# Half of a short convolution on TensorE, and three smaller pieces moved, in a fused attention and feed-forward kernel

## The chip, the cores and the metric

One core of one Trainium2 chip. The metric is the device time of one execution in microseconds, the median of the runs.

## The reference

Input x is 4 batches of 256 tokens by 256 channels. Each layer half starts with a bidirectional weighted scan over time (its keys and values are a second input, `fside`), and the two halves are a state-space block and a quantised feed-forward block:

```python
# scan, for two sets of weights: forward and reverse recurrences a = a*decay + ek*v, b = b*decay + ek
out = sigmoid(r) * (nf + nb - ekv + euk * vf) / max(df + db - ek + euk, 1e-8) * (0.8 + 0.2 * tf)
# state-space block
z, x, B_proj, C_proj, dt_logits = split(u @ in_proj_w)
x = silu(causal_conv1d(x, conv_weight, conv_bias))        # 4 taps, 512 channels
y = ssd(q=elu(C)+1, k=elu(B)+1, v=x, a=exp(-dt*exp(A_log))) + D_param * v      # 8 heads of 64
y = rms_norm(y) * norm_scale * silu(z);  x = x + y @ out_proj_w
# feed-forward, both matmuls with 8-bit activations and ternary weights
h = layer_norm(gelu(silu(bitlinear158(scan2, w1, b1)))) * g + b
x = x + bitlinear158(h, w2, b2)
```

## The kernel before

Every engine has a program of its own, a hand-written list of calls of small functions at the end of its block; semaphores (`wait_ge`, `then_inc`) join them. All order is in these lists and in `HOME`, which says in which of the 8 PSUM banks each piece lies. A batch b is 256 tokens, two tiles c of 128; the feed-forward works on 8 tiles i.

- SP issues the loads, then per batch `spread_sums(b)` (6 small transfers of the running sums), the transposing transfers `turn_q2(i)` and the stores.
- DVE does the scans: `forward(b, w, k)` and `backward(b, w, k)`, w for the two weight sets, k for denominator and numerator; `add_own`, `recip`, `ratio`, and `gated(b)`, which makes uT, the input of the batch's projections. ACT makes the exponentials (`wkv_exp`, `wkv_own`), the decays D and the seed of the reciprocal; POOL multiplies by the values (`times_v`, `own_times_v`).
- PE projects uT: `features(b)` (B, C and dt), `conv_in(b, i)` (x, two channel blocks of 128 each), `gate_in(b, c)` (z). The convolution runs with channels on the partitions: `conv_last_tap` (ACT) writes cv = x times the last tap plus bias, `conv_taps(b, i)` (DVE) adds the three earlier taps in 6 operations for each i, and `conv_turns(b, c)` (PE) turns the 4 blocks of a tile to tokens on the partitions. ACT's `silu_conv` makes vv.
- `softplus_out(b)` (DVE) gives la, the log decays; `running_sums(b)` (PE, ACT, DVE) and `spread_sums(b)` make the operands of `log_decays(b, c, g)` (PE); ACT's `decays` takes the exponential, DVE's `attend` multiplies by the scores.
- `within(b, c)` (PE) first adds the skip (8 matmuls against `skips`, identities scaled by D_param, made once by ACT), then 8 matmuls with dec. `y_turns`, `project(p)` and `residual(p)` end the block. p counts parts: batches 0 to 2, then the last batch's two tiles as parts 3 and 4.
- `norm_h`, `ffn_in_scale`, `quantise_h`, `q1_turns` quantise. `ffn_up(i)` multiplies by w1T and adds the bias through `diag` (POOL, 1/al1 on the diagonal; 1/al1 from DVE's `ffn_in_back`) times b1b, b1 broadcast to 128 partitions. `ffn_silu`, `ffn_gelu`, `ffn_var`, `ffn_center`, `ffn_shift`, `ffn_max`, `ffn_round` follow, then `turn_q2(i)` and `ffn_down(i)`; DVE's `ffn_back(i)` makes the output scale al2.

## Time and profile before

| | |
|---|---|
| median of 3 runs | 205.26 us (204.13 to 205.44) |
| profiled execution, first to last instruction | 201.1 us |
| instructions | 3190 |
| mean granted clock of TensorE | 0.924 |

The time of a run is taken from outside the program, the span inside it; of the profiled execution the span is all that is known. "Busy" is time in which an engine has an instruction under way; for PE the ends of matmuls are modelled, so the distance between starts tells more than the printed duration. A 32-bit matmul shows as two records. The timelines print start, duration, engine, line, operation, output and input tiles, and the idle time before with what ended it.

### The profile page before, as it was taken

Reading aid. Unit: us, or ns where it says so; the run is one execution under the profiler, and the core shown is the slowest. Engines: PE = TensorE matmul, PEld = TensorE weight load, DVE = VectorE, ACT = ScalarE, POOL = GpSimd, SP = SyncE. Lnnn points to the kernel's source line nnn. Section 1 sums busy time; section 2 is a strip of 40 time slices with the busy share of each in tenths; the row PEclk is TensorE's granted clock in tenths of the full one; section 3 lists DMA queues with packets and bytes.
Section 4 is the critical chain, followed back from the end, with each engine's and each line's share of the span. In section 5 each row is a group of like instructions: output and inputs, shape, how many; then the busy total and the mean of one; then the engine's idle time right before and its main releaser. Section 6 shows DMA issues by size and latency. Waiting matters only on the chain.

```text
span 201.1 us, 3190 instructions
## 1 busy us (share of the span) xinstructions
PE 159.6 (79%) x903; PEld 117.4 (58%) x908; DVE 178.6 (89%) x320; ACT 159.8 (79%) x293; POOL 100.3 (50%) x172
## 2 busy tenths in 40 slices
PE   7800039459799999999999999999999999672844
PEld 5600038334589867698757488957668766350633
DVE  2899999999999999899999899979866769998991
ACT  5860599969699279998789999899999886877632
POOL 3609759000426523758700086467455287858570
...
GB/s 133 320 385 382 248 2 104 106 3 2 1 0 3 0 0 2 4 3 0 2 2 3 0 0 3 0 2 0 54 96 14 0 0 0 130 7 49 81 60 96
DMA packets 12304, 11.55 MB, mean 57 GB/s; under 512 B 7680, under 2 KB 10368, under 8 KB 12032
## 3 DMA queue, kind: packets, MB, share of 16 engines
...
q8 instruction: 7, 0.11, 0.2%
...
## 4 chain that ended last, share of the span: by engine, by line
PE 45%; DVE 14%; ACT 12%; issue 12%; POOL 8%; DMA 5%; SPq 3%; POOLq 1%; DVEq 0%; ACTq 0%
PE banks L1688 41%; DVE Ys L1239 5%; DMA wn<-wn 4%; PE banks L1685 3%; DVE Fs L1230 3%; DVE nd L1250 3%; SPq L355 2%; ACT Ys L744 1%; POOL qr L514 1%; ACT Ys L742 1%; POOL wn L576 1%; ACT dec L691 1%; ACT dec L844 1%; ACT D L724 1%; DMA cum_t<-cum_s 1%
## 5 line engine op out<-in xcount | busy, mean ns | idle before, releaser
L1688 PE MATMUL banks<-inw,uT 128*128 128x8 f32 (+1 forms) x64 | 21.7, 465 | 19.4 <-DVE uT L1277 19.4
L1688 PEld LDWEIGHTS banks<-inw,uT 128*128 128x128 f32 x64 | 10.9, 217 | 24.7 <-issue 24.5
L1230 DVE TENSOR_TENSOR_SCAN Fs<-D,E 128x514 f32<-128x514 f32 x16 | 23.0, 1460 | 0.5 <-POOL D L449 0.5
L1688 PE MATMUL banks<-uT,inw 128*128 128x256 f32 x80 | 20.3, 398 | 0.0
L1239 DVE TENSOR_TENSOR_SCAN Ys<-D,Fs 128x514 f32<-128x514 f32 x16 | 19.7, 1250 | 0.0
L1323 DVE SCALAR_TENSOR_TENSOR cv<-banks,cols,cv 128x255 f32<-128x255 f32 (+2 forms) x48 | 19.4, 472 | 0.1
L1688 PEld LDWEIGHTS banks<-uT,inw 128*128 128x128 f32 x80 | 15.2, 197 | 4.2 <-issue 2.1
L508 POOL TENSOR_TENSOR vs<-vv,grow 128x512 f32<-128x512 f32 x4 | 4.5, 1121 | 25.8 <-issue 20.3
L1688 PEld LDWEIGHTS banks<-vv,skips 128*128 128x128 f32 x128 | 15.2, 192 | 1.9 <-issue 1.8
L495 POOL TENSOR_TENSOR own<-own,vT 128x1024 f32<-128x1024 f32 x4 | 12.1, 3025 | 8.4 <-DVE own L1220 8.4
L1688 PE MATMUL banks<-vv,dec 128*128 128x64 f32 x128 | 15.6, 275 | 0.0
L1688 PE MATMUL banks<-vv,skips 128*128 128x64 f32 x128 | 15.3, 273 | 0.0
L1688 PE MATMUL banks<-b1b,diag 128*128 128x512 f32 x32 | 15.0, 592 | 0.0
L1688 PE MATMUL banks<-outw,yzT 128*128 128x256 f32 x64 | 15.0, 382 | 0.1
L1688 PEld LDWEIGHTS banks<-vv,dec 128*128 128x128 f32 x128 | 14.9, 192 | 0.0
L501 POOL TENSOR_TENSOR nd<-nd,Ys 128x512 f32<-128x512 f32 x4 | 5.2, 1301 | 17.5 <-DVE Ys L1261 17.5
L1688 PE MATMUL banks<-w2T,wn 128*128 128x256 f16 x64 | 9.0, 290 | 6.0 <-DMA wn<-wn 6.0
L1688 PE MATMUL banks<-starts 128*128 128x256 bf16 x80 | 12.1, 317 | 1.3 <-POOL starts L429 1.3
L1688 PEld LDWEIGHTS banks<-outw,yzT 128*128 128x128 f32 x64 | 11.8, 190 | 2.3 <-issue 0.5
L742 ACT ACTIVATE Ys<-nd 128x1024 f32<-128x1024 f32 (+1 forms) x5 | 4.4, 885 | 9.9 <-DVE nd L1250 9.9
L930 ACT ACTIVATE wn<-wn,grs 128x1024 f16<-128x1024 f32 x8 | 9.2, 1146 | 2.6 <-DVE wn L1443 1.5
L1347 DVE TENSOR_TENSOR dec<-dec,banks 128x1024 f32<-128x1024 f32 x8 | 9.7, 1210 | 1.7 <-ACT dec L844 1.7
...
## 6 DMA issues: line engine op xcount, KB each, us to landing
...
```

The source lines that it names most:

```text
L495: pool.tensor_tensor(own[:, b % 2, :, 1, :], own_e(b), vT[:, b].unsqueeze(1).broadcast_to([P, 2, CT * T]), ALU.mult)\
L501: pool.tensor_tensor(nd[:, 1, 1], nd[:, 1, 1], rn[:, 1], ALU.mult).then_inc(rat2_ok, 1)
L508: pool.tensor_tensor(by_head(vs[:]), by_head(vv[:, b % 2, 0]), grow[:, 0, :].unsqueeze(2).broadcast_to([P, NH, HD]), ALU.mult).then_inc(vs ...
L742: act.activation(seed, den, ACT.Relu, bias=-DEN_FLOOR).then_inc(rl_ok, 1)
L930: act.activation(Q2[:, i % 2], Y[:, i % 2], ACT.Square, scale=grs[:, i:i + 1], accum_out=qss[:, i:i + 1])\
L1230: dve.tensor_tensor_scan(Fs[:, w, k], D[:, w, 0:CT * TS], E[:, b % 2, k].rearrange("p c t -> p (c t)"), 0.0, ALU.mult, ALU.add).then_inc(f ...
L1239: dve.tensor_tensor_scan(Ys[:, w, k][:, ::-1], D[:, w, 1:CT * TS + 1][:, ::-1], Fs[:, w, k][:, ::-1], 0.0, ALU.mult, ALU.add).then_inc(ys_ ...
L1250: last = dve.scalar_tensor_tensor(nd[:, :, w, s], y, gap[:, w, ct, b:b + 1], own[:, b % 2, w, :, s], ALU.mult, ALU.add)
L1323: dve.scalar_tensor_tensor(cv[:, ft, back:], at("conv_in", b, i)[:, j * T:(j + 1) * T - back], cols[:, w:w + 1], cv[:, ft, back:], ALU.mul ...
L1347: dve.tensor_tensor(dec[:, c], dec[:, c], at("scores", b)[:, c * P:(c + 1) * P].unsqueeze(1).broadcast_to([P, NH, P]), ALU.mult).then_inc( ...
L1685: return pe.transpose(dst, src, ident[0:n, 0:n])
L1688: return pe.matmul(dst, lhsT, rhs, start=start, stop=stop)
```

## The change

- **Convolution.** Channel blocks 2 and 3 (`conv_in(b, 1)`) go another way: ACT copies them raw into `xps`, which has 3 zero columns ahead, and `conv_turns` multiplies shifted slices of xps with `taps`, 8 diagonal matrices made once by POOL, so that the sum over taps and the turn are one accumulation in PSUM; the bias comes in by a matmul of one row of ones with one row `convb`. Blocks 0 and 1 stay as they were.
- **Skip.** POOL multiplies vv by D_param (`skip_values`), and `within` adds it with one matmul of 512 columns against the identity. ACT's `make_skips` goes.
- **Bias of ffn_up.** b1 and the factor 1/al1 are each split in three 16-bit pieces (`bias_piece` on ACT and `bias_rest` on POOL for b1; `bias_factors` on POOL, `factor_turns` on PE, `factor_rows` on ACT for the factor); the product is one 16-bit matmul over 67 rows.
- **Tile scales.** al1 and al2 are made by POOL (in `bias_factors`, `ffn_round`). DVE's `ffn_in_back` and `ffn_back` go. Statistics have a column per tile, so that some waits go.
- **Lists and banks.** All lists and `HOME` are new, the loads' order too. `gate_x` writes over xcT, `crest` shares bcr.

```diff
 HOME = {
-    "conv_turns": ((2, 3), (7, 2), (1, 0), (7, 6)),
+    "conv_turns": ((2, 4), (7, 1), (4, 4), (5, 6)),
...
+            def make_taps():
+                pool.wait_ge(ident_ok, 2)
+                pool.wait_ge(cols_in, 16)
+                for j in range(2):
+                    for k in range(TAPS):
+                        w = R_CV + k * FT + 2 + j
+                        last = pool.tensor_scalar(taps[:, j, k], ident[:], cols[:, w:w + 1], 1.0, ALU.mult, ALU.mult)
+                last.then_inc(taps_ok, 1)
...
+            def bias_factors(p):
+
+                s = tiles_of(p)
+                pool.wait_ge(hr_ok, 2 * p + 2)
+                pool.wait_ge(hq_ok, p + 1)
+                pool.wait_ge(wmean_ok, 3)
+                for i in range(s.start, s.stop):
+                    pool.tensor_scalar(fac[:, i:i + 1], hmv[:, i:i + 1], hr[:, i:i + 1], wrec[:, 0:1], ALU.mult, ALU.mult)
+                    last = pool.tensor_scalar(al1[:, i:i + 1], hm[:, i:i + 1], hr[:, i:i + 1],
+                                              (wmean if i < FIRST_TANH else whalf)[:, 0:1], ALU.mult, ALU.mult)
+                last.then_inc(al1_ok, 1)
+                pool.wait_ge(al1_ok, p + 1)
+                for k in range(3):
+                    n = 6 * p + 2 * k + 2
+                    if k == 0:
+                        pool.tensor_tensor(fact[:, s], fac[:, s], hq[:, s], ALU.mult).then_inc(fac_ok, 1)
+                    else:
+                        pool.tensor_tensor(fact[:, s], fact[:, s], fpc[:, s, 0, k - 1], ALU.subtract).then_inc(fac_ok, 1)
+                    pool.wait_ge(fac_ok, n)
+                    pool.tensor_scalar(fpc[:, s, :, k], fact[:, s].unsqueeze(2).broadcast_to([P, s.stop - s.start, 3]),
+                                       1.0, 0.0, ALU.mult, ALU.add).then_inc(fac_ok, 1)
+                    if k < 2:
+                        pool.wait_ge(fac_ok, n + 1)
...
+            def skip_values(b, c):
+                pool.wait_ge(heads_in, 16)
+                pool.wait_ge(vv_ok, TT * b + c + 1)
+                if b >= 1:
+                    pool.wait_ge(y_ps, TT * (b - 1) + c + 1)
+                pool.tensor_tensor(by_head(skv[:, c]), by_head(vv[:, b % 2, c]),
+                                   heads[:, 2, :].unsqueeze(2).broadcast_to([P, NH, HD]), ALU.mult).then_inc(sk_ok, 1)
...
+            def conv_raw(b):
+                act.wait_ge(xp_ps, 2 * b + 1)
+                act.wait_ge(pads_ok, 1)
+                if b >= 1:
+                    act.wait_ge(cvT_ps, TT * b)
+                act.activation(xps[:, :, PAD:], halves(at("conv_in", b, 1)), ACT.Copy).then_inc(raw_ok, 1)
...
+            def factor_rows(p):
+                s = tiles_of(p)
+                act.wait_ge(fT_ps, p + 1)
+                act.activation(fT[:, s.start * P:s.stop * P], at("factor_turns", p)[0:KB, 0:(s.stop - s.start) * P],
+                               ACT.Copy).then_inc(fT_ok, 1)
...
             def conv_turns(b, c):
+                bank = at("conv_turns", b, c)
+                pe.wait_ge(ones_ok, 1)
+                pe.wait_ge(b_in, 48)
+                pe.wait_ge(taps_ok, 1)
+                pe.wait_ge(raw_ok, b + 1)
+                mm(bank[:, 2 * P:], ones[NS:NS + 1, :], convb, True, False)
+                for j in range(2):
+                    for k in range(TAPS):
+                        mm(bank[:, (2 + j) * P:(3 + j) * P], xps[:, j, c * P + k:(c + 1) * P + k], taps[:, j, k], False,
+                           j == 1 and k == TAPS - 1)
                 pe.wait_ge(ident_ok, 2)
-                pe.wait_ge(tap_ok, 4 * PAD * (b + 1))
-                turn_4(at("conv_turns", b, c), [cv[:, ft, c * P:(c + 1) * P] for ft in range(FT)]).then_inc(cvT_ps, 1)
+                pe.wait_ge(tap_ok, 2 * PAD * (b + 1))
+                for ft in range(2):
+                    last = turn(bank[:, ft * P:(ft + 1) * P], cv[:, ft, c * P:(c + 1) * P])
+                last.then_inc(cvT_ps, 1)
...
             def within(b, c):
                 bank = at("within", b, c)
-                pe.wait_ge(cumi_ok, 2)
+                pe.wait_ge(ident_ok, 2)
+                pe.wait_ge(sk_ok, TT * b + c + 1)
+                mm(bank, ident[:], skv[:, c], True, False)
                 pe.wait_ge(vv_ok, TT * b + c + 1)
-                for h in range(NH):
-                    part = slice(h * HD, (h + 1) * HD)
-                    mm(bank[:, part], skips[:, h], vv[:, b % 2, c, part], h == 0, False)
...
             def ffn_up(i):
...
-                pe.wait_ge(dg_ok, i + 1)
+                pe.wait_ge(fT_ok, part_of(i) + 1)
+                pe.wait_ge(b1_ok, 5)
                 for g in range(2):
                     half = slice(g * 512, (g + 1) * 512)
-                    last = mm(ffn_mid(i)[:, half], diag[:, i % 2], b1b[:, half], False, True)
+                    last = mm(ffn_mid(i)[:, half], fT[:, i * P:(i + 1) * P], b1r[:, half], False, True)
```

PE where batch 0's turns end and batch 1 begins (`taps,xps` are the tap diagonals, `uT,inw` conv_in and the B and C features, `vs,sc` is between). Before:

```order
L1688 MATMUL banks<-never,identb 128x512
L1688 MATMUL banks<-cum_t,cum_s 128x512
L1685 MATMUL banks<-ident,cv 128x128 x4
L1688 MATMUL banks<-never,identb 128x512
L1688 MATMUL banks<-cum_t,cum_s 128x512
L1688 MATMUL banks<-never,identb 128x512
L1688 MATMUL banks<-cum_t,cum_s 128x512
L1688 MATMUL banks<-uT,inw 128x256 x4
L1688 MATMUL banks<-inw,uT 128x8 x4
L1688 MATMUL banks<-uT,inw 128x256 x2
L1688 MATMUL banks<-vv,skips 128x64 x8
L1688 MATMUL banks<-vv,dec 128x64 x8
```

Now:

```order
L1735 MATMUL banks<-bcf,ones 128x256
L1735 MATMUL banks<-taps,xps 128x128 x8
L1732 MATMUL banks<-ident,cv 128x128 x2
L1735 MATMUL banks<-never,identb 128x512
L1735 MATMUL banks<-cum_t,cum_s 128x512
L1735 MATMUL banks<-inw,uT 128x8 x4
L1735 MATMUL banks<-uT,inw 128x256 x10
L1735 MATMUL banks<-vs,sc 128x512
L1735 MATMUL banks<-tri,la 72x128 x2
L1735 MATMUL banks<-bcf,ones 128x256
L1735 MATMUL banks<-taps,xps 128x128 x8
L1732 MATMUL banks<-ident,cv 128x128 x2
```

Each tile's turns now carry the ones row and 8 diagonals; features(1) stands ahead of both conv_in(1, .), and the running sums and first turns of batch 1 come before within(0, 0), not after it.

DVE from the first scan to the first log decays la (`Fs` forward, `Ys` backward scan, `nd` add_own, `tn` and the Ys after it recip, `uT` gated). The first rows before:

```order
L1230 SCALAR_TENSOR_TENSOR Fs<-D,E 128x514
L1173 TENSOR_SCALAR decay<-fdec,eew 128x3 x4
L1180 TENSOR_SCALAR gap<-decay 128x4x3
L1182 SCALAR_TENSOR_TENSOR gap<-decay,gap 128x4x3
L1184 TENSOR_SCALAR gap<-gap 128x4x3
L1230 SCALAR_TENSOR_TENSOR Fs<-D,E 128x514 x2
L1239 SCALAR_TENSOR_TENSOR Ys<-D,Fs 128x514
L1220 TENSOR_SCALAR own<-own 128x2x512
L1239 SCALAR_TENSOR_TENSOR Ys<-D,Fs 128x514
L1230 SCALAR_TENSOR_TENSOR Fs<-D,E 128x514
```

Now:

```order
L1285 TENSOR_SCALAR D<-starts,decay 128x256 x4
L1304 TENSOR_SCALAR E<-E 128x2x256
L1318 SCALAR_TENSOR_TENSOR Fs<-D,E 128x514
L1308 TENSOR_SCALAR own<-own 128x2x512
L1318 SCALAR_TENSOR_TENSOR Fs<-D,E 128x514 x2
L1261 TENSOR_SCALAR decay<-fdec,eew 128x3 x4
L1268 TENSOR_SCALAR gap<-decay 128x4x3
L1270 SCALAR_TENSOR_TENSOR gap<-decay,gap 128x4x3
L1272 TENSOR_SCALAR gap<-gap 128x4x3
L1327 SCALAR_TENSOR_TENSOR Ys<-D,Fs 128x514 x2
```

The minimum of E of batch 1 now stands ahead of the first scan, the own minimum right behind it, and the decays of the other batches behind three scans instead of one.

PE in the tail (`outw,yzT` is project(4), `b1b,diag` and `b1r,fT` the bias of ffn_up, `w2T,wn` ffn_down, `identb,fpc` factor_turns). Before:

```order
L1688 MATMUL banks<-outw,yzT 128x256 x4
L1685 MATMUL banks<-ident,h 128x128 x2
L1688 MATMUL banks<-wcol,less 128x256
L1688 MATMUL banks<-w2T,wn 128x256 x8
L1688 MATMUL banks<-wcol,less 128x256
L1688 MATMUL banks<-w2T,wn 128x256 x8
L1688 MATMUL banks<-w1T,q1T 128x512 x4
L1688 MATMUL banks<-b1b,diag 128x512 x2
L1685 MATMUL banks<-ident,h 128x128 x2
L1688 MATMUL banks<-wcol,less 128x256
L1688 MATMUL banks<-w2T,wn 128x256 x8
```

Now:

```order
L1735 MATMUL banks<-outw,yzT 128x256 x4
L1735 MATMUL banks<-identb,fpc 67x128
L1735 MATMUL banks<-wcol,less 128x256
L1735 MATMUL banks<-w2T,wn 128x256 x8
L1735 MATMUL banks<-w1T,q1T 128x512 x4
L1735 MATMUL banks<-b1r,fT 128x512 x2
L1732 MATMUL banks<-ident,h 128x128 x2
L1735 MATMUL banks<-identb,fpc 67x128
L1735 MATMUL banks<-wcol,less 128x256
L1735 MATMUL banks<-w2T,wn 128x256 x8
L1735 MATMUL banks<-w1T,q1T 128x512 x4
L1735 MATMUL banks<-b1r,fT 128x512 x2
```

Only ffn_down(1) stands between project(4) and ffn_up(6), and ffn_up(7) comes ahead of ffn_down(3).

## Rows read from the trace of the kernel before

**Rows 1.** The page, part 1: busy us of each engine.

```profile
PE 159.6 (79%) x903; PEld 117.4 (58%) x908; DVE 178.6 (89%) x320; ACT 159.8 (79%) x293; POOL 100.3 (50%) x172
```

**Rows 2.** Busy us of PE, PEld, DVE, ACT, POOL by stage; PE clock; DMA.

```profile
56.00:168.70 112.70, 112.08 (x638) 84.54 (x642) 101.24 (x187) 101.13 (x185) 55.81 (x96) 1.00 0.04 8
168.70:201.10 32.40, 18.70 (x124) 12.60 (x124) 26.39 (x49) 18.83 (x33) 20.65 (x47) 0.95 0.27 66
```

**Rows 3.** The chain that ended last: start us, us, what.

```profile
46.42 0.80 SPq L355
...
50.01 1.69 DMA cum_t<-cum_s
...
55.98 14.31 PE banks L1688 x96
```

**Rows 4.** Timeline of PE, 72 to 102 us: start us, us, operation.

```profile
72.82 0.93 PE L1688 MATMUL banks<-bcf 64*128 64x128 f32 x6
73.68 0.39 PE L1688 MATMUL banks<-la,late 128*128 128x8 f32 x2
...
81.05 0.38 PE L1688 MATMUL banks<-never,identb 128*128 128x512 bf16 x1
81.30 0.38 PE L1688 MATMUL banks<-cum_t,cum_s 99*128 99x512 bf16 x1
...
83.82 1.96 PE L1688 MATMUL banks<-uT,inw 128*128 128x256 f32 x8
...
87.37 1.89 PE L1688 MATMUL banks<-vv,skips 128*128 128x64 f32 x16
89.10 1.95 PE L1688 MATMUL banks<-vv,dec 128*128 128x64 f32 x16
...
94.46 1.08 PE L1688 MATMUL banks<-yy,ident 128*128 128x512 f32 x2
95.38 0.60 PE L1685 MATMUL banks<-ident,nd 128*128 128x128 f32 x4
95.81 0.60 PE L1688 MATMUL banks<-tri,la 128*72 128x128 f32 x4
96.25 0.60 PE L1685 MATMUL banks<-ident,h 128*128 128x128 f32 x4
...
101.87 1.88 PE L1688 MATMUL banks<-b1b,diag 128*128 128x512 f32 x4
```

**Rows 5.** Timeline of DVE (and one of ACT), 7 to 88 us.

```profile
7.06 2.34 DVE L1230 TENSOR_TENSOR_SCAN Fs<-D,E 128x514 f32<-128x514 f32 x1 [0.53 <-POOL D L449]
...
7.07 0.63 ACT L703 ACTIVATE E<-vT 128x512 f32<-128x512 f32 x1 [0.28 <-DMA vT<-in_kT_dram]
...
26.84 1.56 DVE L1277 SCALAR_TENSOR_TENSOR uT<-th,nd 128x512 f32<-128x512 f32 x1
...
41.94 0.38 DVE L1311 SCALAR_TENSOR_TENSOR la<-dtp,expa 128x72 f32<-128x72 f32 x2
...
55.17 0.66 DVE L1277 SCALAR_TENSOR_TENSOR uT<-th,nd 128x512 f32<-128x512 f32 x1
...
86.99 2.33 DVE L1230 TENSOR_TENSOR_SCAN Fs<-D,E 128x514 f32<-128x514 f32 x2
```

**Rows 6.** Groups of DVE: busy us, mean ns, idle before.

```profile
L1323 DVE SCALAR_TENSOR_TENSOR cv<-banks,cols,cv 128x255 f32<-128x255 f32 (+2 forms) x48 | 19.4, 472 | 0.1
...
L1464 DVE TENSOR_SCALAR al<-qm,gq,wmean 128x1 f32<-128x1 f32 x8 | 2.0, 266 | 0.0
```

**Rows 7.** POOL: two groups, and one operation of its timeline.

```profile
L508 POOL TENSOR_TENSOR vs<-vv,grow 128x512 f32<-128x512 f32 x4 | 4.5, 1121 | 25.8 <-issue 20.3 <-ACT grow L809 5.5
...
L566 POOL TENSOR_SCALAR gq<-qr,grs 128x1 f32<-128x1 f32 x8 | 2.1, 264 | 0.8
...
26.16 1.70 POOL L488 TENSOR_TENSOR E<-E,vT 128x512 f32<-128x512 f32 x1 [2.35 <-DVE E L1216]
```

**Rows 8.** Timeline of ACT in the tail: tile 7's tanh.

```profile
182.27 1.12 ACT L899 ACTIVATE own<-banks,al 128x1024 f32<-128x1024 f32 x1 [0.84 <-PE banks L1688]
```

More of the change, by code:

```diff
@@ L76, in build @@
     NR = R_CV + TAPS * FT
+    KB = 64 + 3
     with ExitStack() as ctx:
@@ L985, in _ @@
+            features(1)
+            decays(0, 1, 1)
+            softplus_log(1)
+            conv_last_tap(1)
+            conv_raw(1)
+            act.preload_act_table_set("silu_and_others")
             silu_conv(0, 1)
             silu_z(0, 1)
-            cross_scores(0)
+            silu_conv(1, 0)
             act.preload_act_table_set("exp_and_others")
-            decays(0, 0, 1)
-            decays(0, 1, 0)
-            growths(0)
-            wkv_exp(3)
-            features(1)
-            decays(0, 1, 1)
@@ L995, in _ @@
-            conv_last_tap(1, 1)
-            gate_x(2)
-            wkv_own(3)
+            growths(1)
+            cross_scores(1)
+            bias_piece(1)
+            gate_x(2)
+            running_sums(1)
+            gate_x(3)
+            act.preload_act_table_set("natural_log_exp_and_others")
+            recip_seed(2, 0, 2)
+            bias_piece(2)
+            make_turn(3)
+            act.preload_act_table_set("silu_and_others")
+            silu_z(1, 0)
+            silu_conv(1, 1)
@@ L1814, in project, with factor_turns @@
                 last.then_inc(o_ps, 1)
+            def factor_turns(p):
+                s = tiles_of(p)
+                pe.wait_ge(masks_ok, 4)
+                pe.wait_ge(fac_ok, 6 * p + 7)
+                for k, i in enumerate(range(s.start, s.stop)):
+                    last = mm(at("factor_turns", p)[0:KB, k * P:(k + 1) * P],
+                              fpc[:, i].rearrange("p j k -> p (j k)")[:, 0:KB], identb[:], True, True)
+                last.then_inc(fT_ps, 1)
             def q1_turns(p):
@@ new lines, in _ @@
+            log_decays(0, 1, 1)
+            pe.wait_ge(vv_ok, 1)
+            features(1)
+            pe.wait_ge(dex_ok, 3)
+            conv_in(1, 1)
+            pe.wait_ge(zs_ok, 1)
+            conv_in(1, 0)
+            pe.wait_ge(bcr_ok, 2)
+            pe.wait_ge(dtx_ok, 2)
+            between(0)
+            running_sums(1)
+            conv_turns(1, 0)
+            pe.wait_ge(vv_ok, 2)
+            scores(1)
+            pe.wait_ge(vv_ok, 3)
+            r2_turns(1)
+            gate_in(1, 0)
@@ L1896, in _ @@
+            pe.wait_ge(ty_ok, 1)
+            gate_in(1, 1)
             within(0, 0)
-            between(0)
-            pe.wait_ge(dex_ok, 4)
+            conv_turns(1, 1)
+            pe.wait_ge(att_ok, 2)
             within(0, 1)
-            conv_in(1, 0)
+            features(2)
             y_turns(0, 0)
-            gate_in(1, 0)
-            running_sums(1)
-            scores(1)
+            log_decays(1, 0, 0)
+            conv_in(2, 1)
+            pe.wait_ge(yss_ok, 2)
+            pe.wait_ge(yz_ok, 2)
@@ L1951, in _ @@
-            conv_turns(2, 0)
-            pe.wait_ge(dex_ok, 11)
-            conv_turns(2, 1)
-            pe.wait_ge(dex_ok, 12)
-            gate_in(2, 1)
-            within(2, 0)
+            log_decays(2, 1, 1)
+            pe.wait_ge(wcol_ok, 1)
+            gate_in(2, 1)
+            pe.wait_ge(dex_ok, 10)
+            conv_turns(2, 1)
+            pe.wait_ge(dex_ok, 11)
+            within(2, 0)
+            pe.wait_ge(zs_ok, 6)
+            ffn_up(1)
+            between(2)
             pe.wait_ge(vv_ok, 6)
-            between(2)
```

959 lines of the change are left out of this document (464 added, 495 removed).

## The prediction

> **What bounds the kernel now.** I read the page's first part, then the busy time by stage, the chain that ended last, and the timelines of PE and DVE. The page gives DVE 89% of the span, PE and ACT 79% each [rows 1]; by that alone VectorE is the limit, and a change that takes work from it should pay. The stages say otherwise. From 56 to 168.7 us PE is busy 112.08 of 112.70 us at the full clock of 2.4 GHz, while DVE has 101.24 and ACT 101.13 [rows 2]. The chain agrees: from 55.98 us it runs over pieces such as 96 matmuls in a row [rows 3]. So there are three stages. Up to 56 us the DVE's scans decide when PE may start (its last step is uT of batch 1, at 55.17 [rows 5]); then 112.7 us belong to PE; then 32.4 us of tail, in which DVE, POOL, ACT and transfers hand single tiles to each other (DVE 26.39, PE 18.70 busy [rows 2]). The profiled span is 201.1 us; the median of the runs is 205.26, so some 4.2 us lie around it. I sum against the span and add the 4.2 back.
>
> **PE, part by part.** Prices are from start to start in the timeline [rows 4], a "record" being one of the two into which a 32-bit matmul falls.
> - Skip product: 8 matmuls of 64 columns per tile cost 89.10-87.37 = 1.73 us. One of 512 columns against the identity costs what yy,ident costs, 95.38-94.46 = 0.92. That is -0.81, for 8 tiles -6.5.
> - Bias: b1b,diag is printed 1.88 for 4 records, with an overlapped end of 0.16 as in yy,ident (printed 1.08, 0.92 by starts), so 1.72. Two 16-bit matmuls of 512 columns cost about 0.44 to 0.5 (one is 81.30-81.05 = 0.25), and the factor turns 0.11 a tile. That is -1.2, for 8 tiles -9.3.
> - Convolution: per tile two of four turns go (4 records of 128 columns are 95.81-95.38 = 0.43, so -0.22). In come one matmul of 256 columns (2 records at 1.96/8 = 0.245, 0.49) and 8 of 128 columns, 16 records. This is the price that decides. The trace has no such matmul over 128 rows. Below it lie the turns and tri,la (0.43 and 0.44 for 4 records, 0.11 each) [rows 4]; above it lie bcf with 6 records in 73.68-72.82 = 0.86, 0.143 each, and the 256-column record at 0.245. I take 0.115, near the rows with full width; it makes 1.84 a tile and +2.1 net, for 8 tiles +17. With 0.143 it is +20, with 0.245 +33.
> The sum on PE is +17-6.5-9.3 = about +1. The page TensorE: Matmul & The Clock Gate of the Trainium skill (Back-to-back issue gap) gives about 81 ns per matmul of N=128 in a sustained stream; the trace's full-width 32-bit records are slower, 0.11; by the page's figure the 128 added records would be 4 us cheaper in all.
>
> What of this lies in the PE stage? Conv turns of batches 1 to 3 (six tiles, +12.6 to +15), all eight skips (-6.5), biases of tiles 0 to 5 (-7), one warm-up block of 8 matmuls (it lies ahead of the stage), and the turn of ratio 1, now in the stage (+0.4): -0.5 at 0.115, +2 at 0.143. The stage had next to no idle time, so DVE's relief can't shorten it: DVE loses 24 of 48 tap operations (19.4/48 = 0.40 each, -9.7 us) and its small scale operations (8 al2 at 0.25, -2, and 13 for al1 and ral that I price alike, -3) [rows 6], 14 to 15 us in all, hidden behind PE, and ACT's gain (8 last-tap pieces less, 8 skip diagonals less) is taken back by the raw copies, bias pieces and factor rows.
>
> **The front.** Here the new lists matter. Before, the first scan is at 7.06 and la of batch 0 at 41.94 [rows 5], 34.9 us. Laid end to end in the new order: 16 scans at 2.33/2 = 1.17 [rows 5] (18.7), eight pieces around them (own minimum twice 1.2, decays and gaps 1.2, nd 2.6, two reciprocals 2.7, ratio, uT, features 2.1), and 0.3 of waits: 29 us. The difference is stalls that the old order had around the own product on POOL. But the first scan now waits for the minimum of E of batch 1, whose exponential was at 7.07, straight off the transfer [rows 5], and that transfer now has another 256 KB ahead: scan at about 8.7, +1.7. la(0) then comes at about 38, -4. The running sums follow at once (+2.2 of wait for PE and ACT) and the six spreading transfers start near 41.5 instead of 46.42 [rows 3]; they took 5.3 us to 51.7. Gated(1) has one tap group less ahead but two more pieces and a wait for the reciprocal seed; I get 54.1 for 55.8. ACT now makes its table changes one after the other here (silu_conv, growths, silu_z, features, four table loads), so la(1) is at about 61.7 and PE waits some 2 us at the running sums of batch 1. Walking on to where gate_in(1, 1) and conv_turns(1, 1) are done I arrive at 75.2 to 75.7 with 19.4 us of PE work behind, where before it was 19.7 at 75.95. So the front is worth half a microsecond at this point, since PE waits again.
>
> From there PE has 90.2 us to project(4) at 0.115 less what is taken ahead of it (ffn_down(0), q1_turns(3)), before 90.8: the stage ends 0.6 us earlier at the low price, 1.3 later at the high one. I take -0.6.
>
> **The tail.** Tile 6's project(3) stands 10.3 us of PE work ahead of project(4), before 4.3, so ffn_up(6) follows it at once. Tile 7 was the last; its tanh began at 182.27, released by PE [rows 8]. Now its bias factors go through POOL (eight small operations at 0.2 to 0.35 each, as gq's 0.264 [rows 7], about 2.5 us with their waits), one PE turn and an ACT copy that stands behind gelu(6), so ffn_up(7) is done about 1.8 us sooner than those 182.27-168.7 = 13.6 us after project(4); before its tanh ACT now does square(5), so 1.3 of it reaches the end. DVE has 2 us less in this stage, which gives 0.6 more; the al2 product on POOL between the last two roundings takes 0.3 back. Tail: -1.6. The sum is 201.1-0.6-1.6 = 198.9, with the 4.2 about 203.0.
>
> **Rivals.**
> - *DVE was the pace after all* (chance 0.24). PE's fullness would be an effect of matmuls that stretch while they wait. For it: DVE too is 90% busy in that stage, 101.24 of 112.70 us. Against: the same function costs the same on PE wherever its rows stand in the timeline. Half of the 14 us comes through: 201.1-6.5+4.2, about 198.
> - *The 32-bit weight load shows* (0.14, slower). Each added record of 128 columns carries a load of a full 128x128 block, and 0.19 us is what one takes; if it isn't hidden behind so short a matmul, a record costs 0.19: 96 records in the PE stage by 0.075 more is +7.2, some 208.5. For it: bcf at 0.143 is above the turns. Against: skips with 64 columns ran at 0.108 with the same load. It decides from 0.14 on, where the 2.2 us of gain are gone.
> - *POOL becomes a link* (0.14, slower). It gets 8 skip products at 1.12 us [rows 7], which stand between silu and within(b, c), two bias rests of 1024 columns, and five factor chains of 2 to 3.5 us, some 30 us more in a queue in order; clip_weights(1) on DVE sits behind scale_outw and weight_round(1). If each batch loses 1 to 1.5 us of PE to it, 207. While both read two operands, each slows the other: uT took 1.56 us beside POOL's 1.70 us product, 0.66 alone [rows 5, 7]. The Trainium skill's GPSIMD Engine Reference (Engine selection; Key points) warns of this: two-input elementwise work is about half as fast there and contends with VectorE instructions that have two SBUF inputs. The trace agrees.
> - *The front isn't won* (0.08): the first loads or the table changes come later than I put them, and the gain of the tail is all: 205.3 less or more 1.
>
> **How the numbers follow.** My case has 0.40 and its own range of 200.5 to 205.5. A measurement of this kernel tells about 1% from no change, 2 us, so faster is below 203.2: 0.24 of my case, 0.23 of the first rival, 0.01 of the last, 0.48. Slower is above 207.3: 0.02, 0.12 and 0.10, with 0.02 of the last, 0.26. The rest, 0.26, is no change. The range 198.0 to 208.5 leaves out the full gain of DVE's 14 us and a record price above 0.19.
>
> **What would show it.** Right: PE again full from some 54 to 168 us; starts of taps,xps 0.11 to 0.12 apart; la(0) near 38; DVE's busy time in the PE stage down by 10 us or more with the stage's length the same; the last tanh near 181. Wrong: gaps on PE released by POOL skv or by ACT vv; tap records at 0.14 or more; PE with idle time while the span falls by 5 us (then DVE was the pace); a wait of DVE for wn from POOL that PE then feels at project(0) or within(1, 0).

## The result, and the profile after

The changed kernel takes 244.68 us (median of 4 runs, 243.37 to 247.19), before in the same session 204.69 (203.39 to 205.44): the ratio is 1.1945, 95% interval [1.1866, 1.2023]. It is 40 us slower where I had forecast 203.0. The profiled execution has a span of 245.1 us and belongs to the longest of the four runs; the spans of the others are 241.6 to 243.2, so the stages below hold 2 to 3.5 us more than the others', and the gains counted from 244.68 are good to about 1 us.

The page's first part, to be held against [rows 1]:

```profile
PE 173.6 (71%) x879; PEld 125.8 (51%) x884; DVE 168.0 (69%) x276; ACT 160.1 (65%) x289; POOL 142.7 (58%) x237
```

DVE did lose its 10 us (178.6 to 168.0). PE gained 14 us, and POOL 42, part of which, as will be seen, is waiting inside its instructions. The page's time slices show where the time went (busy tenths in 40 slices of 6.1 us; the clock row is the granted one):

```profile
PE   1900009942499999599996089999999998556545
...
POOL 5469004509519043298499961077685888877780
PEclk9985555895558999859999659999999999958777
DMA  6969410000100000200000000000004000130411
```

PE is empty in the third to sixth slice (12 to 37 us; in before from 10 to 25), low from the ninth to the eleventh, and empty once more in the 23rd, in which POOL is full. The transfers at the start go on in a ragged row of 6, 9, 6, 9, 4, 1. The chain that ended last (start, us, what) names the same places:

```profile
5.77 19.91 DMA xcT<-in_xT_dram
...
57.33 7.23 POOL taps L487 x8
...
132.10 8.65 POOL fpc L531
```

In the chain of before no transfer and no group of POOL was longer than 4.2 us. To place the loss I cut each span at two PE instructions, the first of features(1) (inw,uT, 8 records) and the first of project(4) (outw,yzT, 8 records): front, PE stage, tail.

| kernel | front | stage | tail | span |
|---|---|---|---|---|
| before | 57.8 | 109.1 | 34.2 | 201.1 |
| after | 76.1 | 131.0 | 38.0 | 245.1 |

So 18.3 us are lost in the front, 22.0 in the stage (the cut differs from [rows 2] by a few us), 3.8 in the tail. The rows of each place:

The front, ACT and DVE of after:

```profile
25.71 0.63 ACT L819 ACTIVATE xcT<-xcT 128x512 f32<-128x512 f32 x1 [15.83 <-DMA xcT<-in_xT_dram]
...
31.43 0.69 DVE L1346 SCALAR_TENSOR_TENSOR tn<-nd,Ys 128x512 f32<-128x512 f32 x1 [8.05 <-ACT Ys L815]
...
49.83 0.38 DVE L1399 SCALAR_TENSOR_TENSOR la<-dtp,expa 128x72 f32<-128x72 f32 x2
```

gate_x(1) waits until 25.71 for its transfer; behind it in ACT's list stands the seed of the first reciprocal, for which DVE idles 8.05 us. la(0) comes at 49.83 for 41.94 before [rows 5] and 38 in the forecast. The wait is not all of it. Two groups of scans are longer than the 1.17 us apiece of the forecast, and each lies beside POOL's own product:

```profile
10.87 4.44 DVE L1318 TENSOR_TENSOR_SCAN Fs<-D,E 128x514 f32<-128x514 f32 x2
...
42.86 6.79 DVE L1327 TENSOR_TENSOR_SCAN Ys<-D,Fs 128x514 f32<-128x514 f32 x4
...
11.04 3.19 POOL L547 TENSOR_TENSOR own<-own,vT 128x1024 f32<-128x1024 f32 x1 [2.09 <-DVE own L1308]
...
43.07 3.26 POOL L547 TENSOR_TENSOR own<-own,vT 128x1024 f32<-128x1024 f32 x1
```

That is 2.1 us too much in each group. Then POOL and PE:

```profile
57.32 7.23 POOL L487 TENSOR_SCALAR taps<-ident,cols 128x128 f32<-128x128 f32 x8
...
64.80 1.19 PE L1735 MATMUL banks<-bcf,ones 1*128 1x256 f32 x2 [5.13 <-POOL taps L487]
65.92 3.78 PE L1735 MATMUL banks<-taps,xps 128*128 128x128 f32 x16
```

The diagonals stand behind times_v(2), which had waited 9.35 us. The group's line for L487 gives 366 ns for the shortest, 368 median and 2322 for the longest of the eight. After the gap PE runs at the granted clock of 0.5, 1.2 GHz (page slices 9 5 5 5 8): 3.78 us for 16 tap records that take 1.89 at full clock. In the stage:

```profile
126.06 2.41 DVE L1410 SCALAR_TENSOR_TENSOR cv<-banks,cols,cv 128x255 f32<-128x255 f32 x6
128.38 1.22 DVE L1327 TENSOR_TENSOR_SCAN Ys<-D,Fs 128x514 f32<-128x514 f32 x1
129.52 1.20 DVE L1318 TENSOR_TENSOR_SCAN Fs<-D,E 128x514 f32<-128x514 f32 x1
130.64 0.67 DVE L1454 TENSOR_TENSOR yy<-banks,zs 128x512 f32<-128x512 f32 x1
...
132.33 1.21 DVE L1327 TENSOR_TENSOR_SCAN Ys<-D,Fs 128x514 f32<-128x514 f32 x1
...
137.94 2.70 DVE L1338 SCALAR_TENSOR_TENSOR nd<-Ys,gap,own 128x512 f32<-128x512 f32 x4
...
128.38 2.41 POOL L519 TENSOR_SCALAR fac<-hmv,hr,wrec 128x1 f32<-128x1 f32 x1
...
131.48 0.23 POOL L531 TENSOR_SCALAR fpc<-fact 128x6 bf16<-128x6 f32 x1
...
132.10 8.64 POOL L531 TENSOR_SCALAR fpc<-fact 128x6 bf16<-128x6 f32 x1
```

Two instructions of the same form, six elements a partition: 0.23 us at 131.48, 8.64 at 132.10. The long one begins as DVE enters an unbroken row of scans and sums and ends at 140.74, when that row ends (137.94+2.70 = 140.64). The 2.41 us of fac at 128.38 cover two scans and end as DVE turns to an instruction that reads PSUM. PE waits 8.77 us for it.

### The profile page after: what moved, and what is told of

It reads as the page before. It is cut to its first block, busy times and chain, and to the rows that moved or that the text cites. A ratio compares the mean times of both kernels' runs of the same rounds, so it can differ in the third digit from the quotient of the medians.

```text
span 245.1 us, 3178 instructions
## 1 busy us (share of the span) xinstructions
PE 173.6 (71%) x879; PEld 125.8 (51%) x884; DVE 168.0 (69%) x276; ACT 160.1 (65%) x289; POOL 142.7 (58%) x237
## 3 DMA queue, kind: packets, MB, share of 16 engines
q1 hardware_dynamic: 11782, 11.09, 15.3%
HBM read 8.44 MB, written 1.05 MB: 39 GB/s over the span
## 4 chain that ended last, share of the span: by engine, by line
PE 30%; POOL 24%; issue 13%; DVE 11%; ACT 10%; DMA 9%; SPq 2%; POOLq 1%; DVEq 0%; ACTq 0%
PE banks L1735 28%; DMA xcT<-in_xT_dram 8%; POOL fpc L531 5%; POOL taps L487 3%; POOL own L547 3%; PE banks L1732 2%; POOL fac L519 2%; DVE Ys L1327 1%; DVE nd L1338 1%; DMA wn<-wn 1%; POOL h L598 1%; POOL wn L633 1%; DVE banks L1507 1%; POOL E L540 1%; SPq L320 1%
## 5 line engine op out<-in xcount | busy, mean ns | idle before, releaser
L1735 PE MATMUL banks<-uT,inw 128*128 128x256 f32 x80 | 23.4, 446 | 0.0
L1735 PEld LDWEIGHTS banks<-uT,inw 128*128 128x128 f32 x80 | 17.6, 226 | 4.7 <-issue 1.2
L1735 PEld LDWEIGHTS banks<-taps,xps 128*128 128x128 f32 x128 | 18.0, 224 | 3.3 <-issue 3.3
L1735 PE MATMUL banks<-taps,xps 128*128 128x128 f32 x128 | 19.6, 316 | 0.0
L1735 PE MATMUL banks<-w2T,wn 128*128 128x256 f16 x64 | 12.2, 355 | 4.5 <-DMA wn<-wn 4.5
L1374 DVE SCALAR_TENSOR_TENSOR bcf<-banks,bcr 64x256 f32<-64x256 f32 x8 | 3.4, 421 | 15.8 <-ACT bcr L835 15.6
L1465 DVE SCALAR_TENSOR_TENSOR x<-banks,yr,xn 128x256 f32<-128x256 f32 x8 | 3.6, 480 | 15.3 <-PE banks L1735 15.3
L1338 DVE SCALAR_TENSOR_TENSOR nd<-Ys,gap,own 128x512 f32<-128x512 f32 x16 | 13.5, 897 | 0.0
L1346 DVE SCALAR_TENSOR_TENSOR tn<-nd,Ys 128x1024 f32<-128x1024 f32 (+1 forms) x5 | 5.0, 1007 | 11.9 <-ACT Ys L815 11.9
L819 ACT ACTIVATE xcT<-xcT 128x512 f32<-128x512 f32 x4 | 2.5, 622 | 15.8 <-DMA xcT<-in_xT_dram 15.8
L531 POOL TENSOR_SCALAR fpc<-fact 128x6 bf16<-128x6 f32 (+1 forms) x15 | 11.9, 797 | 1.4
## 6 DMA issues: line engine op xcount, KB each, us to landing
inw<-in_in_w_dram SPq DMA_DIRECT2D x1, 1160.0 KB, 20.5
```

Source lines behind the costliest of these rows:

```text
L531: pool.tensor_scalar(fpc[:, s, :, k], fact[:, s].unsqueeze(2).broadcast_to([P, s.stop - s.start, 3]), 1.0, 0.0, ALU.mult, ALU.add).then_in ...
L1338: last = dve.scalar_tensor_tensor(nd[:, :, w, s], y, gap[:, w, ct, b:b + 1], own[:, b % 2, w, :, s], ALU.mult, ALU.add)
L1346: dve.scalar_tensor_tensor(tn[:, w0:w1], nd[:, 0, w0:w1], DEN_FLOOR, rd[:, w0:w1], ALU.max, ALU.mult)\
L1735: return pe.matmul(dst, lhsT, rhs, start=start, stop=stop)
```

## The experiments

Labels e and h change the kernel after, f the kernel before, g goes from e8 back. The medians of before that were measured beside them are 203.8 to 204.9 us. "Front, stage, tail" are cut as above. Each quoted block is what I expected before the run.

**Three waits mended one by one.** e1 moves one ACT call (which costs two more table loads), e2 one POOL call, e3 adds memsets on DVE, e4 is all three.

```diff
 e1, ACT:   gate_x(0)
-           gate_x(1)
            ...
            recip_seed(0, 1, 2)
            ...
+           gate_x(1)
 e2, POOL:
+           make_taps()
            times_v(2)
-           make_taps()
 e3, DVE:   backward(3, 0, 1)
+           rest(0)      # dve.memset(pause[:, 0:1], 0.0)
            forward(3, 1, 0)
+           rest(1)
            ...
```

> One part of the new ACT list undone: gate_x(1), which waited for the DMA of xcT until 25.71 us and held the seed of the first reciprocal behind it, stands behind recip_seed(0,1,2) again, with the table loads it needs there (two more, 1.28 us each, on ACT). Theory (the front is lost to one queued wait): DVE's idle 8.05 us before tn at 31.43 shrinks to under 2.5 us, uT(0) comes near 29.5 to 31 instead of 35.89, la(0) near 44 instead of 49.83, and the total falls by 3 to 6 us from 244.7. Rival (the front is lost to the loads themselves, or what is won there is taken back by the taps' wait at 57 to 65): uT(0) moves by less than 2 us, or it moves and the total falls by less than 1.5 us.

> Only POOL's list changes: make_taps stands ahead of times_v(2) instead of behind it, where POOL was idle 9.35 us. Theory A (POOL is starved of a port that it shares with DVE, and the eight products took 7.23 us because of that): beside the scan block 43 to 49.5 they take 4 us or more as well, but end before 56; the wait of PE on taps (5.13 us) goes, features(1) starts 4 to 6 us sooner than 76.06, and the total falls by 4 to 7 us. Theory B (each such product simply takes 0.9 us on POOL): the same 7.2 us for eight, ended by 54, the same gain. What tells A from B is the spread of the eight durations: A has 0.3 to 0.4 us for those beside an idle DVE or one that reads PSUM and over 1 us beside scans, B has 0.9 for each. Theory C (the wait at 59.6 hid another, such as cv0 or tap): PE's gap stays over 3 us and the total moves by less than 1.5 us.

> After with six one-column memsets of 0.1 us put on DVE between the scans and sums of 132 to 141 us (after backward(3,0,1), forward(3,1,0), forward(3,1,1), backward(3,1,0), backward(3,1,1), add_own(3,0)). Theory A (POOL's tiny fpc instruction of 8.64 us waited for the shared port, which DVE's instructions with two SBUF inputs handed to each other without a gap; a memset, which reads nothing, lets POOL in): the 8.64 us falls below 3 us, PE's wait of 8.77 us to under 3, and the total falls by 5 to 8 us although DVE has six instructions more. Theory A2 (the port is what POOL waits for, but a memset doesn't hand it over): fpc stays near 8.6 and ends where DVE's block ends. Rival B (the 8.64 us is a hiccup of POOL itself, such as loading code, not DVE's doing): it stays as long at the same place whatever DVE runs, and its end no longer falls together with the end of DVE's block.

> The edits of e1, e2 and e3 together. Theory (the 40 us are a few queued waits, each about 5 to 9 us, and all the arithmetic of the change was priced nearly right): the three add up, 244.7 falls to 222 to 230. Rival (each gain runs into the next wait of the same chain): under 10 us in all, 235 or more.

e1: 237.12 us, -7.6, more than expected; uT(0) at 28.60, la(0) at 44.47. e2: 240.43, -4.3; the eight durations are 368 ns at the shortest, 392 median, 1299 the longest, 5.57 us in all: theory A's spread, not B's. e3: 247.43, no gain, and its rows are A2's:

```profile
132.64 8.79 POOL L532 TENSOR_SCALAR fpc<-fact 128x6 bf16<-128x6 f32 x1
...
134.01 1.21 DVE L1322 TENSOR_TENSOR_SCAN Fs<-D,E 128x514 f32<-128x514 f32 x1
134.02 0.06 DVE L1233 MEMSET pause<- 128x1 f32 x1
...
140.61 0.73 DVE L1342 SCALAR_TENSOR_TENSOR nd<-Ys,gap,own 128x512 f32<-128x512 f32 x1
```

The memset is printed beside the scan, not between two; POOL's instruction ends at 141.43, DVE's row at 141.34. It had moved with DVE's row, which speaks against a hiccup of POOL. e4: 234.58, 10 us less, so the theory missed and the rival is all but met: e3's part gave nothing, and e1 and e2 don't quite add up.

**The port opened.** e5 is e1 and e2 with DVE's PSUM work first and the scans behind a wait; h2 is that edit alone in after.

```diff
             conv_taps(2)
+            norm_gate(1, 1)
+            running_sums(2)
+            dve.wait_ge(fac_ok, 7)
             backward(3, 0, 0)
             forward(3, 0, 1)
-            norm_gate(1, 1)
-            running_sums(2)
             backward(3, 0, 1)
```

> After with the edits of e1 and e2, without the memsets of e3, and DVE's list in another order: running_sums(2) and norm_gate(1,1), which read PSUM, come right behind conv_taps(2), and the seven scans and four sums of batch 3 start only when POOL's bias_factors(0) is done (a wait on its semaphore). Theory A (POOL's tiny instructions starve behind DVE's unbroken row of instructions with two SBUF inputs): no instruction of bias_factors(0) takes over 1.5 us, PE's wait of 8.9 us goes, DVE's scans start 1 to 4 us later, and the total is 5 to 9 us under e4's 234.6, so 226 to 230. Rival B (a hiccup of POOL that has nothing to do with DVE): an instruction of 8 us still stands in bias_factors(0), now with DVE waiting as well, and the total is 235 or more.

> After with nothing but e5's edit of DVE's list: norm_gate(1,1) and running_sums(2) ahead of the scans of batch 3, and these behind bias_factors(0). Theory (the starved factor chain is a loss of its own): no POOL instruction of 8 us in it, PE's wait of 8.8 us gone, 8 to 11 us under after, 234 to 237. Rival (it pays only where the front is mended too): under 4 us.

e5: 224.22 us, ratio 1.098 [1.0899, 1.106], 10.4 under e4 though DVE now waits 0.71 us. h2: 235.42, ratio 1.1535 [1.141, 1.1661], 9.3 under after, as its theory had it; POOL's chain takes 0.20 to 0.35 us an instruction, and PE's wait is gone. In e5 the same chain, beside DVE's reads of PSUM:

```profile
115.64 0.23 POOL L531 TENSOR_SCALAR fpc<-fact 128x6 bf16<-128x6 f32 x1
115.96 0.20 POOL L529 TENSOR_TENSOR fact<-fact,fpc 128x2 f32<-128x2 f32 x1
116.24 0.31 POOL L531 TENSOR_SCALAR fpc<-fact 128x6 bf16<-128x6 f32 x1
...
118.47 1.39 POOL L574 TENSOR_TENSOR yr<-ymv,mhalf 128x1 f32<-128x1 f32 x1
```

The last row shows what happens as soon as the scans begin (117.18): 1.39 us for an operation of 0.55. So the cause is shown as far as the order goes: with DVE's row of scans and sums beside it POOL's instruction waits for the row's end, and without it there is no wait. That two inputs from SBUF are what matters fits every row here, but no run changed that alone. The Trainium skill (SBUF — State Buffer, "SBUF: two separate sides") has the lock: a DVE instruction with two SBUF inputs and a GpSimd instruction that reads SBUF exclude each other for their whole length. The traces agree, and show in addition that the loser can miss its turn through a whole row.

**Each part alone, in before.** f1 takes the skip product, f2 the bias by rows, f3 the taps. f2 and f3 had a mistake of mine in them: load_lng waited for uT(1) ahead of spread_sums(0) in SP's list, and PE waited 11.9 and 10.8 us for cum_t. f2c and f3b put it behind; f2c also loads b1 to 128 rows (next paragraph). To make room, all of these but f1 also write gate_x over xcT, as the change does.

```diff
 f1  within:   -  mm(bank[:, part], skips[:, h], vv[:, b % 2, c, part], h == 0, False)   # 8 of these
               +  mm(bank, ident[:], skv[:, c], True, False)
 f2c ffn_up:   -  mm(ffn_mid(i)[:, half], diag[:, i % 2], b1b[:, half], False, True)
               +  mm(ffn_mid(i)[:, half], fT[:, i * P:(i + 1) * P], b1r[:, half], False, True)
 f3b conv_turns as in the change; conv_taps(b, 1) goes; POOL: own_times_v(1), make_taps()
```

> The kernel before with the skip part alone: POOL multiplies vv by D_param, within adds it with one matmul of 512 columns against the identity, make_skips goes. All lists stay, the eight products stand where POOL was idle or behind state_values. Theory (my price of the skip holds, 0.81 us less on PE per tile, and POOL hides its products): 4 to 6.5 us faster, 198 to 201. Rival (POOL becomes a link, each product of about 1.04 us or more beside DVE delays state_values, times_v or the norms): no gain, 203 to 208.

> The kernel before with the bias part alone: b1 and 1/al1 in three 16-bit pieces, the product by one 16-bit matmul over 67 rows instead of a 32-bit one against diag. 1/al1 still comes from DVE's ffn_in_back, so POOL has six tiny instructions per part instead of a diagonal per tile. Theory (my price holds, 1.2 us less on PE per tile): 5 to 9 us faster, 196 to 200. Rival (the chain of factor, its turn, its copy and the matmul is late, as at 132 to 141 us in after): one wait of PE over 2 us on fpc or fT, and no gain, 203 or more.

> The kernel before with the convolution part alone: blocks 2 and 3 by diagonals on PE, make_taps on POOL where it was idle 16 us, all other lists kept. Theory (PE sets the pace from 56 to 168.7 us, my price of 2.1 us a tile holds, and what DVE gets back hides behind PE): 12 to 17 us slower, 217 to 222. Rival (DVE was the pace, its 24 operations less bring 10 us): 195 to 203.

> The bias part alone in before, as f2, without f2's two accidents: b1 is loaded to 128 rows, and load_lng (which I had made to wait for uT(1)) stands behind spread_sums(0), which it had held up by 10 us. Theory (PE 1.15 us less a tile, no new wait over 2 us): 196 to 201. Rival (the new chains of tiny instructions on POOL and the copies on ACT make waits that eat it): 203 to 208.

> The convolution part alone in before, as f3, with load_lng behind spread_sums(0). Theory (2.55 us a tile on PE as e5's rows show, eight tiles, PE bound from 56 us on; make_taps' 8.28 us of POOL stand where nothing waits, ffn_diag's 8.48 us in f3 may recur): 19 to 22 us slower than before, 223 to 227. Rival (part of it hides in PE's waits, since DVE has 24 instructions less): 212 to 220.

| run | us | ratio, 95% | front, stage, tail |
|---|---|---|---|
| f1 | 206.52 | 1.0132 [1.0039, 1.0225] | 57.8, 112.2, 34.2 |
| f2 | 235.57 | 1.1524 [1.1445, 1.1603] | |
| f3 | 234.08 | 1.1474 [1.1373, 1.1576] | |
| f2c | 218.84 | 1.0731 [1.0664, 1.0797] | 59.7, 113.9, 42.2 |
| f3b | 220.90 | 1.0838 [1.0784, 1.0892] | 63.0, 122.0, 33.9 |

No part wins. In f1 PE's skip records fell from 15.3 to 8.5 us, and yet the stage got 3 us longer: PE's busy time in it went from 108.5 to 104.1 us, its idle time from 0.6 to 8.0. Two of its DVE rows say why:

```profile
55.79 1.22 DVE L1238 TENSOR_TENSOR_SCAN Fs<-D,E 128x514 f32<-128x514 f32 x1
56.93 2.00 DVE L1247 TENSOR_TENSOR_SCAN Ys<-D,Fs 128x514 f32<-128x514 f32 x1
...
58.99 1.86 DVE L1238 TENSOR_TENSOR_SCAN Fs<-D,E 128x514 f32<-128x514 f32 x1
```

Both took 1.2 us in before; beside them POOL's first two products took 4.31 us. So POOL costs DVE time as well, and PE then waited for DVE: 1.51 and 1.12 us on dec, 1.03 on la. It also waited 1.6 us in all for POOL's products themselves. DVE's busy time in the stage rose by 3.7 us (97.7 to 101.4), about what the stage gained. So with less work PE no longer sets the pace alone. How far DVE would let it go without the new products on POOL is not shown, since every part that takes work from PE adds some to POOL.

f3b is the other side. It adds work to PE, and all of it comes through: busy 121.8 of 122.0 us, 13.3 more than in before, and the stage is 12.9 longer, while DVE is busy 6.7 us less for nothing. Its 16.4 us are under the 19 to 22 of its theory and near the +17 of the prediction. f3b also has the starved instruction with no bias part in it at all: ffn_diag's second product took 8.48 us, 0.37 in before. f2c missed both its ranges, most of it in the tail, where PE waits 2.83 us for fpc and a group w2T,wn of 1.05 us takes 1.89.

**The load of 67 rows.** f2 showed it: in_w (the row inw<-in_in_w_dram) landed 22.9 us after its issue, in before 10.8, in f3 11.5. The one early load that f2 changes is b1's, from 128 rows to 67. e7 is after with this line:

```diff
-                sp.dma_start(b1f, b1.unsqueeze(0).broadcast_to([KB, NI])).then_inc(b_in, 16)
+                sp.dma_start(yzT[:].rearrange("p c a t -> p (c a t)"), b1.unsqueeze(0).broadcast_to([P, NI])).then_inc(b_in, 16)
```

> After with one word changed: b1 is loaded to all 128 partitions of its tile instead of 67 (512 KB instead of 268; only 67 rows are used, as before). In f2, whose only new load has 67 rows, in_w landed 22.9 us after its issue instead of 10.8 in the kernel before, and 11.5 in f3, which loads 128 rows. Theory (a transfer of 67 rows runs on one of the 16 DMA engines, since 67 has no divisor up to 16, and whatever later load has a share on that engine waits some 10 us; this, not the place of load_xT(1) in the list, is why xcT came at 25.7): in_w lands in about 11 us, gate_x(1) starts before 20 us, DVE's 8.05 us at 31.43 go, and the total falls by 7 to 11 us, so 234 to 238, as in e1 or better, at twice the bytes. Rival (the loads are late because of their order and number): the doubled bytes make it the same or up to 1.5 us later, 244 to 247.

e7: 235.50 us, ratio 1.1554 [1.1493, 1.1614], 9.2 us less for twice the bytes; DVE's wait of 8.05 us is gone. Issues of after, then of e7 (KB, median us from issue to landing), and gate_x(1) in e7:

```profile
wn<-in_w_dram SPq DMA_DIRECT2D x2, 1024.0 KB, 18.9
inw<-in_in_w_dram SPq DMA_DIRECT2D x1, 1160.0 KB, 20.5
```

```profile
wn<-in_w_dram SPq DMA_DIRECT2D x2, 1024.0 KB, 11.3
inw<-in_in_w_dram SPq DMA_DIRECT2D x1, 1160.0 KB, 8.0
```

```profile
13.36 0.63 ACT L819 ACTIVATE xcT<-xcT 128x512 f32<-128x512 f32 x1 [3.77 <-DMA xcT<-in_xT_dram]
```

The Trainium skill (DMA: Bandwidth & Descriptors, "Why a DMA increments its semaphore by 16 and not by 1") has the rule: the transfer is split over the largest number up to 16 that divides its rows, and for 67 that is 1. The times agree; which engines carried it no view here shows. In e7 la(0) comes at 42.55, not at 38: the stretched scans remain.

**All mended, and what is left.** e8 is e5 with e7's line and two fillers on PE in its idle time ahead of log_decays(0, 0, 0). h1 is e8 with gate_x(1) where the change put it.

```diff
             pe.wait_ge(cum_ok, 1)
+            warm(10)     # bank 6, 8 matmuls of 256 columns
+            warm(10)
             log_decays(0, 0, 0)
```

> e5 with the 128 rows of e7 and with two fillers (8 matmuls of 256 columns each) on PE ahead of log_decays(0,0,0), where PE sat idle 4.84 us for cum_t and then ran at 1.2 GHz (granted clock 0.5; taps,xps x16 3.78 us instead of 1.89). Theory (each is a term of its own): the fillers give 2 to 3 us, the load another 1 to 3 beyond what e1's edit had already won, so 218 to 222 against e5's 224.2. Rival (what e1 cured was the same loss, and PE's start is set by DVE's running sums, not by its clock): 223 to 225.

> e8 without e1's edit: gate_x(1) stands on ACT where the change put it, ahead of the first reciprocal's seed. Theory (e1 and e7 cured one and the same loss, the 67-row load): gate_x(1) starts near 13.4 us as in e7, two table loads of 1.28 us fewer on ACT, and the total is within 1.5 us of e8's 219.2. Rival (two losses): 3 us or more above it.

e8: 219.21 us, ratio 1.0745 [1.0662, 1.0829]; front 61.6, stage 120.1, tail 37.0. It is within the 218 to 222 expected; how much of the 5 us under e5 is the fillers' and how much the load's was not parted. h1: its median is 222.63, but its four runs fall in two pairs. Two have e8's granted clock (0.898 and 0.891) and take 219.30 and 220.92 us, about 1 us above e8 and so within the 1.5 of the theory; two have 0.853 and 0.860 and take 224.3 and 224.6. gate_x(1) starts at 13.34. So e1 and e7 most likely cured one loss; on two runs this is not firm.

**The convolution undone.** g1 is e8 with all four blocks through DVE's taps again; g2 is g1 with quantise_h(4) ahead of ffn_round(3) on POOL.

```diff
 g1, DVE:
-            conv_taps(b)
+            conv_taps(b, 1)
+            conv_taps(b, 0)
```

> e8 with the convolution part undone: all four blocks go through ACT's last tap, DVE's earlier taps and PE's turns again, make_taps goes, weight_sums stands behind conv_turns(0,0); skip, bias, tile scales and the new lists stay. Theory A (what is left of e8's 14.7 us is the price of the taps on PE, 2.55 us a tile by e5's rows, while DVE at 73% busy has room for the 24 operations): 13 to 18 us less, 201 to 206, level with before. Rival B (the lists of after don't fit DVE's 24 operations more, 9.7 us, which then stand on DVE's path up to 100 us): 209 to 216.

> g1 with one call of POOL moved: quantise_h(4) ahead of ffn_round(3), 1.1 us of POOL that stood between PE's q1_turns(4) and its input (wait of 3.61 us on h in e8). Theory (POOL, busy without a gap from 170 to 200 us in e8, sets the tail): 1 us less than g1. Rival (ffn_round(3) is as urgent as quantise_h(4)): the same as g1 within 0.5 us.

g1: 229.15 us (1.1217 [1.114, 1.1293]), 10 us more than e8 where theory A expected 13 to 18 less; B's direction, and worse. PE's timeline has the reason, four times over (2.48 and 2.69 us for the last two batches):

```profile
54.12 1.09 PE L1721 MATMUL banks<-ident,cv 128*128 128x128 f32 x4 [1.58 <-DVE cv L1394]
...
74.19 0.63 PE L1721 MATMUL banks<-ident,cv 128*128 128x128 f32 x4 [2.81 <-DVE cv L1394]
```

and the windows give its stage the granted clock 0.88, the third number from the end:

```profile
60.80:188.40 127.60, 113.44 (x527) 80.74 (x533) 106.14 (x170) 101.21 (x183) 80.49 (x134) 0.88 0.06 14
```

In the new lists each conv_turns(b, 0) stands where DVE is late, so the second tap group (2.42 us) is on the path every time, and the granted clock is lower (1.00 in e8's stage), so that PE is busy 113.4 us there, 1.3 more than in e8, with less to do; its idle time is 6.2 more. The taps on PE cost PE, but in these lists they buy DVE's time where it is short. g2: 229.69, no gain; its rival holds.

**The bias part where PE alone should pace.** f2d takes rows for tiles 0 to 5 only and makes b1's pieces at other times.

> The bias part in before for tiles 0 to 5 alone (tiles 6 and 7, in the tail, keep the diagonal); b1's pieces are made from a second load into R2 later, where POOL was idle and not beside the scans of batch 1. Theory (PE alone sets the pace from 110 us on, there 1.15 us less a tile count; f2c lost in the tail, whose length went from 34.2 to 42.2 us, and 1.9 us on DVE at 36): the stage from features(1) to project(4) shrinks from 109.1 to 103 to 106 us, the tail stays near 34, total 199 to 202, faster than before. Rival (the first half is set by DVE as much as by PE, as f1 showed, and the second half's gain is taken by waits for fpc and fT): 204 to 208.

f2d: 211.76 us (1.0395 [1.0314, 1.0476]); front 59.0, stage 114.5, tail 36.4. The theory falls, and the time is above the rival's range too: PE is busy 6 us less in the stage, and the stage is 5.4 longer. Its PE rows show new waits of 1.65 and 1.61 on fpc, 0.81, 1.33 and 0.89 on the copy fT, and la(1) is at 74.34 for 71.34. It also loads b1 a second time, which was not tried alone.

No version beat before, and none of these runs points to one.

## Why the prediction was wrong, point by point

- *"PE full from 56 to 168.7, so the stage belongs to PE and DVE's relief hides."* Half true of before. Work added to PE comes through whole and DVE's relief hides (f3b). But full busy time on PE doesn't say that work taken from it comes back: f1 took some 7 us of records and lost 3 us, because DVE, 90% busy there, is late as soon as something costs it a microsecond, and POOL's new products do. My rival *DVE was the pace* gave this only as a gain.
- *PE's prices.* Right. These are the groups of PE between the two cuts, before first, then e5 (printed busy us, mean ns), and one tile's convolution in e5:

```profile
L1688 PE MATMUL banks<-vv,skips 128*128 128x64 f32 x128 | 15.3, 273 | 0.0
...
L1688 PE MATMUL banks<-b1b,diag 128*128 128x512 f32 x24 | 11.3, 592 | 0.0
...
L1685 PE MATMUL banks<-ident,cv 128*128 128x128 f32 x24 | 3.4, 277 | 0.3 <-ACT dec L844 0.3
```

```profile
L1738 PE MATMUL banks<-taps,xps 128*128 128x128 f32 x96 | 12.3, 281 | 0.0
...
L1738 PE MATMUL banks<-skv,ident 128*128 128x512 f32 x16 | 8.2, 593 | 0.0
...
L1738 PE MATMUL banks<-bcf,ones 1*128 1x256 f32 x12 | 4.1, 424 | 0.0
...
L1738 PE MATMUL banks<-b1r,fT 67*128 67x512 bf16 x12 | 3.6, 379 | 0.0
...
L1735 PE MATMUL banks<-ident,cv 128*128 128x128 f32 x12 | 2.3, 272 | 0.0
...
L1738 PE MATMUL banks<-identb,fpc 128*67 128x128 bf16 x6 | 0.8, 220 | 0.0
```

```profile
60.62 0.69 PE L1738 MATMUL banks<-bcf,ones 1*128 1x256 f32 x2
61.25 2.05 PE L1738 MATMUL banks<-taps,xps 128*128 128x128 f32 x16
63.14 0.38 PE L1735 MATMUL banks<-ident,cv 128*128 128x128 f32 x2
63.35 0.38 PE L1738 MATMUL banks<-never,identb 128*128 128x512 bf16 x1
```

  By printed time, skip is 8.2-15.3 = -7.1, bias 3.6+0.8-11.3 = -6.9 for six tiles, convolution 12.3+4.1+2.3-3.4 = +15.3 for six tiles. Printed durations overlap at their ends, and the forecast went by starts. So measured, the convolution's tile is 63.35-60.62 = 2.73 us for 0.43 before, +2.30 (forecast 2.1; the bias row takes 0.63 where I put 0.49), and six tiles are +13.8. By starts a skip product takes 0.86 us in e5 for 1.73 to 1.80 in before, a bias product 0.44 and its turn 0.06 for 1.72 to 1.81, which makes about -7 and -7.5 (-6.5, -7). The sum is -0.7, where the forecast had -0.5. The tap record at 0.118 (16 in 1.89 us) answers the rival of the weight load: it did not show. That rival's own sum was off: 203.0+7.2 is 210.2, not 208.5.
- *"First scan at 8.7, la(0) at 38, gated(1) at 54.1."* This is the first step that failed. The first scan came at 9.14; la(0) came at 49.83. I put "0.3 of waits" on a stretch in which 8.05 us of wait appeared, and I put every scan at 1.17 us, where two groups beside POOL's own product took 4.2 us more than that. I had written that the new order was rid of the stalls around the own product; it isn't, and even with the loads mended (e7) la(0) is at 42.55, no sooner than in before. My rival *the front isn't won* named late loads at 0.08 and priced them at nothing but the lost gain. The row count of b1's load was in the diff, and I had no term for it (e7: 9.2 us).
- *make_taps* has no term in the prediction; I had taken it for eight short instructions on an idle engine. The median is 0.368, but its place behind a wait made it late (e2: 4.3 us), and what followed ran at half clock.
- *POOL becomes a link* (0.14): the second step that failed. It had the right mechanism, with uT's 1.56 us beside POOL's 1.70 as its row, and the wrong size. I took "each slows the other" as a fraction, 1 to 1.5 us per batch. It is an exclusion, and a tiny instruction inside the factor chain, which I priced at 2 to 3.5 us in all, can lose 8.6 us to it (h2: 9.3 us).
- *The tail, -1.6.* It was +3.8. POOL's instructions follow each other without a gap from 200 to 221 us, PE waits 3.64 us for h and 1.75 for fpc, and its granted clock in the tail is 0.78 for 0.95 in before. The factor chain (2.4 us) was counted once, not behind the rounding of tile 3 and the quantising of tile 7.
- *The sum.* e7's 9.2, h2's 9.3 and e2's 4.3 make 22.8 of 40 us; e8 has 25.5 mended. e8's span is still 17.6 us above before's: 3.8 in the front, 11.0 in the stage, 2.8 in the tail. In e8's stage PE is busy 112.1 us for 108.5 in before's, of which the three parts account for -0.7 (by starts) to 1.3 us (printed), and the rest are pieces that the new list has put between the cuts; the other 7.3 us are idle time, 2.33 us on uT and 1.86 on zs the longest. That this is the new lists' order is my reading, not shown by a run. So some 15 us of the 40 have no proven cause.
